# Graph attention on one core: VectorE's load of the block numbers moves behind the product and the weighting

## The reference: what is computed

```python
q = (x[src] @ qW).reshape(e, 4, 24)
k = (x[dst] @ kW).reshape(e, 4, 24)
v = (x[dst] @ vW).reshape(e, 4, 24)
exp_s = exp(clip(einsum('ehd,ehd->eh', q, k), -10, 10))
norms = segment_sum(exp_s, src)[src]
res = segment_sum((exp_s / (norms + 1e-8))[:, :, None] * v, src).reshape(n, 96)
out = layernorm(x + (x + res))
```

## Time and profile before

| | us |
|---|---|
| median of three runs | 1249.44 |
| the profiled execution's own time | 1251.4 |
| its span, first to last instruction | 1249.6 |
| VectorE busy | 1028.5 (82%) |
| TensorE busy | 968.9 (78%) |
| GpSimd busy | 883.9 (71%) |
| ScalarE busy | 615.4 (49%) |

### The profile page before, as it was taken

The page is one execution under the profiler, slowest core; times in us unless marked ns, Lnnn a source line. Parts: engine busy times, 40 slices in busy tenths (PEclk is TensorE's granted clock), DMA queues, the critical chain, the costliest instruction groups (busy, mean ns, idle before and its releaser), DMA issues.

```text
span 1249.6 us, 22903 instructions
## 1 busy us (share of the span) xinstructions
PE 968.9 (78%) x6512; PEld 880.5 (70%) x6513; DVE 1028.5 (82%) x3139; ACT 615.4 (49%) x1328; POOL 883.9 (71%) x887
## 2 busy tenths in 40 slices
PE   8876787688886888768988867889777787888870
PEld 6765676578775887657888756788667677777760
DVE  7999898899989999888999887999766765555557
ACT  7852584248732598222887322788433332222225
POOL 1317777777777777777777777777777777777752
PEclk9996699659975699775899665899867866555555
DMA  6202222222222222222222222222522222222222
GB/s 174 89 9 71 77 80 74 66 74 80 78 77 70 77 78 77 73 77 70 77 78 79 71 76 73 78 77 80 152 76 80 77 76 78 77 79 76 79 61 77
DMA packets 67240, 98.33 MB, mean 79 GB/s; under 512 B 33127, under 2 KB 53204, under 8 KB 67134
## 3 DMA queue, kind: packets, MB, share of 16 engines
q0 software_dynamic: 41040, 84.10, 24.6%
q1 hardware_dynamic: 26094, 12.94, 3.7%
HBM read 89.77 MB, written 7.22 MB: 78 GB/s over the span
## 4 chain that ended last, share of the span: by engine, by line
DVE 43%; issue 18%; POOL 16%; PE 13%; DVEq 7%; ACT 2%; DMA 1%; SPq 0%; POOLq 0%; ACTq 0%
POOL kv L510 16%; DVE acc L1191 10%; DVEq L425 6%; DVE prod L1210 5%; DVE place_m L1125 4%; PE ps_r L666 4%; DVE wv L1220 4%; DVE score L1230 2%; PE ps_q L652 2%; DVE steps_m L871 2%; DVE place_m L1132 2%; PE ps_a L635 2%; DVE place_m L1129 1%; DVE ohb L1199 1%; DVE clipped L1238 1%
## 5 line engine op out<-in xcount | busy, mean ns | idle before, releaser
L510 POOL DMA_INDIRECT kv<-kv_table,dst_s x855 | 858.5, 1004 | 303.6 <-issue 299.1
L666 PE MATMUL ps_r<-wv,oneh 128*128 128x100 f32 x1752 | 328.3, 354 | 104.1 <-DVE wv L1220 103.1
L652 PE MATMUL ps_q<-qt,onehT 128*128 x1760 | 316.9, 344 | 100.5 <-ACT onehT L775 93.9
L666 PEld LDWEIGHTS ps_r<-wv,oneh 128*128 128x128 f32 x1752 | 298.0, 260 | 127.9 <-DVE wv L1220 125.7
L652 PEld LDWEIGHTS ps_q<-qt,onehT 128*128 128x128 f32 x1760 | 289.1, 252 | 124.1 <-issue 124.0
L727 ACT ACTIVATE steps_m<-iota_f,pos_t 125x254 f16<-125x254 f32 (+4 forms) x652 | 255.9, 482 | 12.1 <-PE ps_b L635 8.6
L1191 DVE TENSOR_TENSOR acc<-acc,ps_r 128x100 f32 x876 | 220.1, 251 | 29.4 <-PE ps_r L666 3.6
L1210 DVE TENSOR_TENSOR prod<-ps_q,kv 128x480 f32<-128x480 f32 x176 | 115.0, 653 | 153.8 <-DMA kv<-kv_table,dst_s 91.2
L775 ACT ACTIVATE onehT<-ps_t 128x640 f32<-128x640 bf16 x176 | 124.0, 705 | 217.9 <-PE ps_t L678 211.4
L768 ACT ACTIVATE wv<-clipped 128x20 f32<-128x20 f32 x176 | 38.5, 219 | 351.1 <-DVE clipped L1238 350.7
L781 ACT ACTIVATE oneh<-ohb 128x640 f32<-128x640 bf16 x176 | 164.5, 935 | 0.9 <-PE ps_r L666 0.9
(11 more groups left out here) (212 smaller groups left out, 692.9 us busy)
## 6 DMA issues: line engine op xcount, KB each, us to landing
kv<-kv_table,dst_s POOLq DMA_INDIRECT x855
kv_table<-kv SPq DMA_DIRECT2D x7, 672.0 KB, 3.4
acc<-in_x_dram SPq DMA_DIRECT2D x6, 336.0 KB, 8.4
steps_m<-in_x_dram SPq DMA_DIRECT2D x6, 336.0 KB, 5.2
out_dram<-kv SPq DMA_DIRECT2D x6, 336.0 KB
dst_i<-in_dst_dram SPq DMA_DIRECT2D x1, 415.0 KB
src_i<-in_src_dram SPq DMA_DIRECT2D x1, 346.7 KB
acc<-in_x_dram SPq DMA_DIRECT2D x1, 288.0 KB, 4.4
```

Of the source, the lines that this page charges most:

```text
L510: nc.gpsimd.indirect_dma_start(kv[:, nm, u, :], None, kv_dram, bass.IndirectOffsetOnAxis(ap=dst_s[:, n * U + u:n * U + u + 1], axis=0)).th ...
L652: last = nc.tensor.matmul(ps_q[nm % 2][:, u * D:(u + 1) * D], onehT[:, nm % 2, u * P:(u + 1) * P], qt[:, bass.ds(blks[u], 1), :].rearrange ...
L666: last = nc.tensor.matmul(to, oneh[:, nm % 2, u, :], wv[:, nm % 2, u, :], start=True, stop=True)
```

## The change

In VectorE's `tiles`, the load of the block numbers that the additions need is issued behind the product and the weighting, ahead of the wait for TensorE's sums. Before, it was issued ahead of the product. The last two iterations, which have an order of their own above these lines, and the loads into `coming` stay as they are.

```diff
--- before.py
+++ after.py
@@ -1255,11 +1255,10 @@
                     return
                 if isinstance(m, int) and m == NBT - 2:
                     coming[m - 1] = blocks_of(mybir.EngineType.DVE, m - 1)
-                if there(m - 2):
-                    blks = blocks_of(mybir.EngineType.DVE, m - 2)
                 multiply()
                 weigh()
                 if there(m - 2):
+                    blks = blocks_of(mybir.EngineType.DVE, m - 2)
                     dve.wait_ge(s_res, m - 2 + 1)
                 if mid:
                     reduce()
```

## The result

The changed kernel takes 1263.39 us (median of five runs, 1260.91 to 1265.19) against 1249.44 us: the ratio of the two is 1.0099, with a 95% interval of 1.0072 to 1.0125. It is slower by 1%, or 13.9 us, and outside the predicted range of 1243.5 to 1252.5. The profiled execution has a span of 1263.4 us, 13.8 us over the one before.

A forecast was written before the change was run, and what follows sets the result against it. The prediction took GpSimd's stream of gathers to bound the kernel: 1249.44 us less 2.2 us from GpSimd's three gaps, all other terms 0, gave 1247.2 us, with a range of 1243.5 to 1252.5.

The forecast's parts named there:

- What bounds: Whole kernel: GpSimd's stream of gathers runs without a pause for 1121 of 1249.6 us, waiting only 2.3 us for others.
- (a): Sorting iterations: the load stays hidden, cost 0, gain 0; where the product waits for its data, the price of (b).
- (b): Ranking iterations and loop: new gap of some 0.35 us behind the weighting; VectorE gains 18 to 23 us by 886 us.
- (c): VectorE's saved 20 us: it catches up with the gathers, and waits for their data grow by about that much.
- (d): GpSimd's three gaps over 0.4 us: the change takes out 1.12 to 2.3 us, taken as 2.2.
- (e): The last iterations: the moved load does not delay the end; cost 0, bound 0 to +0.4 us.
- the open term: The gathers' own length: stretched gathers fall otherwise against ranking work, some 2 to 3 us either way; the largest uncertainty.
- the prediction's own sign of being wrong: Profile after: long GpSimd idle gaps, gathers' busy time over 4 us off 858.5, or span down 10 us or more.
- denser VectorE stretches the gathers: Ranking iterations: without the gap ahead of the product, gathers take longer; 1253.3 or 1256.4 us, chance 0.17.

The follow-up runs named there:

- experiment 7: Kernel before, plus VectorE waits on its own last result between the selections and behind every sixth mark: 1258.18 us, ratio 1.006.
- experiment 2: Kernel before, with the load moved behind the weighting everywhere except in ranking iterations: 1244.94 us, ratio 0.9946.
- experiment 3: Changed kernel a second time: the extra unused load ahead of the product in ranking iterations was dropped at the build; 1262.3 us, ratio 1.0091.
- experiment 4: Kernel before, with ten tiny memsets on GpSimd ahead of the first gather: 1251.79 us, ratio 1.0005.
- experiment 5: Changed kernel, with a second, used load ahead of the product in ranking iterations, beside the one behind the weighting: 1251.7 us, ratio 1.001.
- experiment 1: Kernel before, with the load moved behind the weighting in ranking iterations alone: 1256.48 us, ratio 1.0047.
- experiment 8: Changed kernel, with the one-hot built ahead of the reduction in sorting iterations: 1259.29 us, ratio 1.0053 to the kernel before.
- f3: Changed kernel, with VectorE waits on its own work behind every sixth mark alone: 1257.90 us, ratio 1.0063 to the kernel before.
- f4: Changed kernel, with only a VectorE wait on its own work ahead of the product in ranking iterations, no load: 1248.10 us, ratio 0.9969 to the kernel before.
- experiment 6: Changed kernel, plus VectorE waits on its own last result between the selections and behind every sixth mark: 1244.72 us, ratio 0.9942 to the kernel before.
- experiment 9: Changed kernel, with VectorE waits between selections and behind every sixth mark, and the one-hot ahead of the reduction in sorting iterations: 1244.16 us, ratio 0.994.
- experiment 10: Changed kernel, with VectorE waits on its own work between the selections alone: 1248.17 us, ratio 0.9981 to the kernel before.

## Why the prediction was wrong

**What bounds: right.** The stream of gathers sets the time in every kernel here but that of experiment 7, which shows the limit: only as long as nobody behind it starves it. The conclusion drawn from it, that a faster VectorE can take at most 2.3 us out, was too narrow: the gathers' own length is on the path too, and it moves both ways (experiment 2 is 0.5% faster than the kernel before, with 4.4 us less in the gathers).

**(a) Sorting iterations: half right.** In the first stretches the load runs 1.37 us ahead of the product and is hidden. Where the product waits for its data, the case that I had set aside with the price of (b), it is exposed by 0.28 us. I booked that as time of VectorE, which has time to spare there. Its real price was that it moved the one-hot onto a gather.

**(b) Ranking iterations: right in kind.** 46.5 to 0.7 us ahead of the product; 74 new waits of 0.25 us behind the weighting, where I had said 40 to 50 of 0.35. Where the product has waited for its data the load starts 0.02 us behind it, in the loop 0.1 to 0.24 us, not 0.14.

**(c) Right in kind:** VectorE's waits for data grow by 45.5 us and not by 20. With the gathers 17 us longer there is that much more to wait for, and the 14.2 us that the product had waited for TensorE (`ps_q`) went the same way. **(d)** gave 2.1 us for 2.2. **(e)** gave 0.

**The step that failed is the open term,** "some 2 to 3 us either way" for the gathers' own length. It measured +16.9 us, and the prediction's own sign of being wrong, a gathers' time off by over 4 us, came with it. I had treated it as a redraw: each gather falls elsewhere, single events cancel. For chance alone that holds: 3 to 4 us between traces (experiments 3 and 4). The change did more. It takes the idle time out of ranking iterations, and experiment 5, which puts idle time back with a load, has the stretching of before (28.6 against 31.0 us, 40.6 changed). It isn't a draw of the single run either: in the four kernels with a load ahead of the product there (before, experiments 2, 4 and 5) the gather that starts in the first selection behind the clipping (119.25 and 119.05 above) takes 1.30 to 1.31 us, in the six without one and without waits between the selections (changed, experiments 1, 3 and 8, f3, f4) it takes 5.43 to 5.44.

The rival "denser VectorE stretches the gathers" was the right one, with the chance 0.17, and too cheap: it gave 1253.3 or 1256.4. I priced it by a gather that lost 0.54 us beside a product, and that was misread. One row ahead of those shown stands what held it:

```profile
241.97 1.23 DVE L1068 TENSOR_TENSOR place_m<-steps_m,kb_m 125x910 uint16<-125x910 f16 x2
```

The second of these two selections ends at 243.20, and the gather of 242.53 at 244.02, 0.82 us later; the product had no part in it. The row to price it by stood in the same group, the gather of 4.89 us: not many small losses but nine gathers over 2 us where there were four, and on top 8.0 us in sorting iterations that I had not thought of, most of them beside the one-hot.

The Trainium skill, SBUF - State Buffer, "Who interferes with whom", makes the product harmless to a gather, and the trace agrees: the gather held at 119.05 had been let go at 123.66, 0.6 us ahead of the product, and that of 239.91 (5.01 us, to 244.92) was let go at 244.10, while the product of 244.02 ran. My inference, that a gap filled by the product costs the gathers nothing, doesn't follow. It looks at the product alone. Behind it stands the weighting, with `kv` and `wv` both in SBUF, and 69 gathers before and 51 after ended 0.82 us behind one; five of the latter started beside the product, where a ranking stretch goes over into sorting, and were held for 1.75 us, as none was before. And it looks at the gap alone: with something ahead of the product again, the kernel was 12 and 15 us faster (experiments 5 and 12). The section also says, of VectorE's two-port modes, that the loser blocks for the whole of the other's instruction. The gathers of 1.0 to 1.3 us fit that. That one is held over thirteen instructions (5.43 us) goes beyond it.

**What stays open.** Which gather is held over a whole row and which only to the end of one instruction. The examples all start in the first selection behind the clipping: 0.09 us into it one took 1.31 us (119.25, before), 0.21 us into it one took 5.43 us (119.05, changed), and 0.10 us into it one took 5.01 us (239.91, changed). No rule of the start alone fits these three. So I can say that VectorE's waits inside its rows shorten the gathers (experiments 6, 7 and 9 to 11), but not compute how many are held in a given order. Nor is it settled how the gap ahead of the product does it, or whether the gap does it at all: its removal also moves every later gather against the ranking work, and no experiment parts the two. A held gather was let go with the product right behind the row and no gap (that of 239.91), a gap of 0.04 us (f4) brought as much as one of 1.1 us (experiment 5), and experiment 5 still has the gather of 5.01 us. With the sorting iterations of f4 an unknown part of both gains is the way in which the gathers happened to fall.

## What to carry to other kernels

When one engine's stream sets the time and its instructions take longer beside another engine's, an edit of that other engine's order is not free, even if it removes only idle time. Look at the longest instructions of the stream, ask what ended them, and price the change by these and not by the mean. Then give the stream its openings on purpose: in the changed kernel, waits of VectorE on its own last result inside its long rows of SBUF instructions brought 18.7 us. With that done the moved load paid (13.5 us). But to leave the load alone in ranking iterations and move it elsewhere (experiment 2) came to the same 1244.9 us with no waits at all. So test such an edit stage by stage, and together with what it collides with.

## What the runs showed of the hardware

A gather by indirect DMA of 0.947 us was held for up to 5.44 us beside rows of VectorE instructions on 16-bit data in SBUF, and ended 0.82 us behind the moment of its release. A wait of VectorE on its own last result left 0.03 to 0.04 us between two instructions that follow at once (experiment 6), and none where a short addition ran in between; in the two kernels with such waits no gather took over 2.28 us (experiment 6) and 1.68 us (experiment 7). In the kernel before, a gather that started beside the one-hot alone, counted by the instruction that runs 0.13 us behind its start, ended 0.82 us behind it in 72 of 77 cases, and beside the weighting in 60 of 98 (inputs in SBUF); beside the product, the reduction or the sort's lines 1125, 1129 and 1132 it did in none of 258 (at most one input in SBUF). A load of five block numbers took 1.18 or 0.59 us on VectorE's sequencer, and behind a product that waited for its data it began 0.02 us after the product's start.
